# Moving the attention's loads to GpSimd's queue and its outputs to SyncE's, with an earlier copy and a later turn of the maxima

## The reference

```python
def reference(...):
    x = _layernorm(x + _L0_attn_ref(x, ...))      # sampled values, squeeze-excite gate, silu(out @ w_out)
    x = _layernorm(x + _L0_ffn_ref(x, ...))
    return x

def _L0_ffn_ref(x, ...):
    x = x + _msa(_layernorm(x, ln1_w, ln1_b), w_qkv, w_proj)
    x = x + _moe_mlp(_layernorm(x, ln2_w, ln2_b), gate_w, gate_b, w1, w2)
    return x

def _msa(x, w_qkv, w_proj):                       # 16 heads of 16 channels
    attn = softmax(q @ k.T / sqrt(16), axis=-1)
    return (attn @ v) @ w_proj
```

## Time and profile before

| | |
|---|---|
| median of three runs | 1563.61 us (1557.06 to 1567.67) |
| the profiled execution's own time | 1563.61 us |
| its span | 1561.0 us |
| granted PE clock, mean | 0.968 |
| busy share of the span: PE, DVE, ACT, POOL | 93%, 81%, 65%, 24% |
| attention block | 522 to 1189 us of the span |

### The profile page before, as it was taken

The page is one execution under the profiler, slowest core; times in us unless marked ns, Lnnn a source line. Parts: engine busy times, 40 slices in busy tenths (PEclk is TensorE's granted clock), DMA queues, the critical chain, the costliest instruction groups (busy, mean ns, idle before and its releaser), DMA issues. The chain is left out here.

```text
span 1561.0 us, 31581 instructions
## 1 busy us (share of the span) xinstructions
PE 1453.5 (93%) x11706; PEld 895.9 (57%) x11706; DVE 1264.0 (81%) x2433; ACT 1016.9 (65%) x1705; POOL 371.0 (24%) x633
## 2 busy tenths in 40 slices
PE   7688989998999999999999999999997769999997
PEld 7465656565655344444444444444444649999996
DVE  6889999964566799999999999999962867777773
ACT  3689999963433488888888888888885522222221
POOL 3011111103111012222222222222222732222222
PEclk9789999999999799999999999999998989999999
DMA  3300101014885544433444443443332775656561
GB/s 115 95 8 15 46 20 48 15 62 169 284 255 198 148 82 97 98 91 91 91 92 95 95 88 80 88 91 81 75 91 73 240 258 206 204 205 213 199 215 48
DMA packets 147303, 185.99 MB, mean 119 GB/s; under 512 B 68288, under 2 KB 99008, under 8 KB 147152
## 3 DMA queue, kind: packets, MB, share of 16 engines
q1 hardware_dynamic: 126896, 157.27, 35.8%
q0 software_dynamic: 19280, 26.46, 5.5%
q10 hardware_dynamic: 976, 0.24, 0.1%
HBM read 129.67 MB, written 54.21 MB: 118 GB/s over the span
## 5 line engine op out<-in xcount | busy, mean ns | idle before, releaser
L1684 ACT ACTIVATE at_p<-at_pst 128x512 f32<-128x512 f32 x1024 | 555.0, 597 | 101.8 <-PE at_pst L1732 82.5
L1696 DVE TENSOR_REDUCE at_mx<-at_pmx 128x2 f32<-128x1024 f32 x488 | 576.3, 1215 | 32.1 <-PE at_pmx L1723 29.6
L1748 PE MATMUL at_pacc<-at_p,at_v 128*32 128x256 f32 (+1 forms) x3840 | 324.1, 410 | 2.5 <-ACT at_p L1684 0.2
L1723 PE MATMUL at_pmx<-at_k,at_q 48*128 48x512 f32 x976 | 247.3, 503 | 2.8 <-PEq L1204 2.0
L1732 PE MATMUL at_pst<-at_q,at_k 50*128 50x512 f32 x1024 | 231.1, 409 | 5.1 <-ACT at_p L1684 5.0
L1723 PEld LDWEIGHTS at_pmx<-at_k,at_q 48*128 48x128 f32 x976 | 91.9, 185 | 213.8 <-issue 128.0
L878 PE MATMUL ws_pA<-ident,ws_A 128*128 128x128 f32 x1088 | 152.6, 288 | 23.9 <-ACT ws_A L660 21.6
L1732 PEld LDWEIGHTS at_pst<-at_q,at_k 50*128 50x128 f32 x1024 | 155.5, 188 | 30.4 <-ACT at_p L1684 24.2
L878 PEld LDWEIGHTS ws_pA<-ident,ws_A 128*128 128x128 f32 x1088 | 122.7, 146 | 84.1 <-ACT ws_A L660 37.7
L2251 DVE STREAM_TRANSPOSE ex_zr<-ex_row 32x64 f32<-32x64 f32 x608 | 143.2, 236 | 15.1 <-DMA ex_row<-scratch_routed 7.3
L1748 PEld LDWEIGHTS at_pacc<-at_p,at_v 128*32 128x32 f32 x3840 | 76.9, 108 | 131.4 <-ACT at_p L1684 83.9
(11 more groups left out here) (269 smaller groups left out, 1612.3 us busy)
## 6 DMA issues: line engine op xcount, KB each, us to landing
ex_w<-in_L_ffn_w SPq DMA_DIRECT2D x39, 1024.0 KB, 5.6
at_q<-scratch_qs SPq DMA_DIRECT2D x192, 64.0 KB, 3.1
at_k<-scratch_ks SPq DMA_DIRECT2D x192, 64.0 KB, 3.2
ex_row<-scratch_routed SPq DMA_DIRECT2D x39, 258.0 KB, 5.0
scratch_qs<-gp_split SPq DMA_DIRECT2D x16, 512.0 KB, 3.8
scratch_ks<-gp_split SPq DMA_DIRECT2D x16, 512.0 KB, 4.5
scratch_v<-gp_v SPq DMA_DIRECT2D x8, 1024.0 KB, 5.9
at_v<-scratch_v SPq DMA_DIRECT2D x32, 256.0 KB, 3.9
```

What stands on the lines that cost most here:

```text
L1684: a.activation(pt[:, n % BUFS, k % 2, :], pst[(w * 2 * STEPS + k) % BANKS][:], ACT.Exp).then_inc(exped, 1)
L1696: v.reduce_max(mx[w % 2][:].rearrange("p (h n) k -> p h n k", h=2)[:, :, j // 2, j % 2], pmx[n % SLOTS][:], AX.X).then_inc(taken, 1)
L1723: last = nc.tensor.matmul(pmx[n % SLOTS][:, h, :], att.rows(qst[u], h, ROWS)[:, nt * P:(nt + 1) * P], att.rows(kst[u], h, ROWS)[:, kh * HA ...
L1748: last = nc.tensor.matmul(out, vst[u][:, t, h, :], pt[:, n % BUFS - p + first:n % BUFS + 1, h, c * QUARTER:(c + 1) * QUARTER], start=(s == ...
```

## The change

It has these parts.

- The loads of q, k and v in `attention` move from SP's stream to POOL's. In `gate_and_project` the loads of units 0 and 1 stay on SP and count on semaphores of their own (`att.first`).
- `fold`, `spread` and `store` move from POOL's stream to SP's; `normalise` stays on POOL, behind the loads. SP's order in a unit is now `fold`, `load_w2` or `pad`, `spread`, `store_top`, `store`, all but `store_top` for the unit before. In the next block, `spread` and `store` of the last unit stand on SP ahead of the loads of chunks 2 and 3.
- `TURN` goes from 8 to 9, so `EARLY` from 16 to 14: at the end of `gate_and_project` there are 14 early maxima, spread 1, 1, 1, 1, 4, 4 over the six parts in place of 2, 2, 2, 2, 3, 3 (behind two ahead of them).
- `COPY` goes from 4 to 2.
- PE's wait for the rows of maxima stands ahead of the step's maxima matmuls.
- ACT's first exponential, SP's units and POOL's further loads wait until y0, v and the split q and k of all chunks are stored. The load of the Exp table at the end of `gate_and_project` moves behind the two copies of v.

The diff (only shifts of lines and repeated head lines are left out):

```diff
--- before.py
+++ after.py
@@ -1083,7 +1083,7 @@
     PIECES = 2 * BT
     MAXIMA = 2 * PIECES
     TOPS = 3
-    TURN = 8
+    TURN = 9
     Q = 32
     EARLY = 2 * (2 * BT - TURN)
     LOADS = 2 * 2 * len(STACK) * 16 + 16
@@ -1093,13 +1093,13 @@
 
         return a[h * self.BASE:h * self.BASE + n]
 
-    def load(self, eng, u, of_q, of_k):
+    def load(self, eng, u, of_q, of_k, loaded):
 
         for h in range(2):
             for n, (pq, pk) in enumerate(self.STACK):
                 at = slice(h * self.BASE + n * DK, h * self.BASE + (n + 1) * DK)
-                eng.dma_start(self.qst[u][at, :].bitcast(F32), of_q(pq, h)).then_inc(self.ld[u], 16)
-                eng.dma_start(self.kst[u][at, :].bitcast(F32), of_k(pk, h)).then_inc(self.ld[u], 16)
+                eng.dma_start(self.qst[u][at, :].bitcast(F32), of_q(pq, h)).then_inc(loaded, 16)
+                eng.dma_start(self.kst[u][at, :].bitcast(F32), of_k(pk, h)).then_inc(loaded, 16)
 
     def tops(self, dve, w):
 
@@ -1129,7 +1129,7 @@
     a.vst = [sb(f"at_v{i}", [P, BT, 2, 2 * DK]) for i in range(a.RING)]
     a.mx, a.top_ = [sb(f"at_mx{i}", [P, a.PIECES, 2]) for i in range(2)], sb("at_top", [P, a.PIECES])
     a.top2, a.turned = [sb(f"at_top2{i}", [P, a.Q], F32R) for i in range(2)], [sb(f"at_topT{i}", [P, a.Q]) for i in range(2)]
-    a.ld = [sem(f"at_load{i}") for i in range(a.RING)]
+    a.first, a.ld = [sem(f"at_first_load{i}") for i in range(2)], [sem(f"at_load{i}") for i in range(a.RING)]
     a.y0_out, a.v_out, a.split_out = sem("gp_y_out"), sem("gp_v_out"), [sem(f"gp_split_out{i}") for i in range(4)]
     a.one_rows, a.red, a.mxmm, a.topT, a.split = (sem("at_" + n) for n in ("ones", "reduced", "maxima", "topT", "top_split"))
     a.top_out, a.rows_in = sem("at_top_out"), sem("at_top_rows")
@@ -1233,9 +1233,9 @@
                 sp.wait_ge(att.one_rows, 2 * att.RING)
                 def part(d):
                     return lambda n, h: d[n, (2 * u + h) * DK:(2 * u + h + 1) * DK, 0:L]
-                att.load(sp, u, part(dr["qs"]), part(dr["ks"]))
+                att.load(sp, u, part(dr["qs"]), part(dr["ks"]), att.first[u])
                 sp.dma_start(att.vst[u][:].rearrange("p t h d -> p t (h d)"),
-                             dr["v"][0:L, u * (4 * DK):(u + 1) * (4 * DK)].rearrange("(t p) n -> p t n", p=P)).then_inc(att.ld[u], 16)
+                             dr["v"][0:L, u * (4 * DK):(u + 1) * (4 * DK)].rearrange("(t p) n -> p t n", p=P)).then_inc(att.first[u], 16)
 
             def chunk(i, prev):
                 if i + 1 < CHUNKS:
@@ -1323,9 +1323,9 @@
             ahead(a, chunk)
             for q in range(4):
                 top(CHUNKS - 1, q)
-            nc.scalar.activation(warm[:], hb2[:, 0:1], ACT.Exp)
             for q in range(4, 6):
                 values(CHUNKS - 1, q)
+            nc.scalar.activation(warm[:], hb2[:, 0:1], ACT.Exp)
 
         @block.vector
         def _(dve):
@@ -1401,9 +1401,8 @@
             peak(att.MAXIMA + 1)
             for q in range(4):
                 low(CHUNKS - 1, q)
-                peak(att.MAXIMA + 2 + 2 * q)
-                peak(att.MAXIMA + 3 + 2 * q)
-            for n in range(10, att.EARLY):
+                peak(att.MAXIMA + 2 + q)
+            for n in range(6, att.EARLY):
                 peak(att.MAXIMA + n)
 
         @block.gpsimd
@@ -1492,7 +1491,7 @@
                 w, m = n // att.MAXIMA, n % att.MAXIMA
                 nt, kh, h = m // 4, m // 2 % 2, m % 2
                 if m == 0:
-                    pe.wait_ge(att.ld[w], att.LOADS)
+                    pe.wait_ge(att.first[w], att.LOADS)
                 if w:
                     pe.wait_ge(silu3, CHUNKS)
                     if m >= 3:
@@ -1548,7 +1547,7 @@
             n = att.MAXIMA + 2
             for q in range(PARTS):
                 parts(CHUNKS - 1, q)
-                for _ in range(2 if q < 4 else 3):
+                for _ in range(1 if q < 4 else 4):
                     peak(n)
                     n += 1
 
@@ -1568,7 +1567,7 @@
     TOTAL = (UNITS - 1) * STEPS - EARLY
     BANKS, SLOTS, BUFS = 3, 2, 4
     LAG = 2
-    COPY = 4
+    COPY = 2
     INVERT = 6
 
     qst, kst, vst, mx = att.qst, att.kst, att.vst, att.mx
@@ -1595,18 +1594,6 @@
 
         @block.sync
         def _(sp):
-            def load(w):
-
-                b, pair, u = w // (H // 2), w % (H // 2), w % RING
-                if pair in (0, 2):
-                    for done in [att.v_out] + att.split_out:
-                        sp.wait_ge(done, 16 * (L // HALF) * (b + 1))
-                def part(d):
-                    return lambda n, h: d[n, (2 * pair + h) * DK:(2 * pair + h + 1) * DK, b * L:(b + 1) * L]
-                att.load(sp, u, part(dr["qs"]), part(dr["ks"]))
-                sp.dma_start(vst[u][:].rearrange("p t h d -> p t (h d)"),
-                             dr["v"][b * L:(b + 1) * L, pair * (4 * DK):(pair + 1) * (4 * DK)].rearrange("(t p) n -> p t n", p=P)).then_inc(ld[u], 16)
-
             def load_w2(w):
 
                 i, q, hc = w // RING, w % RING // 2, HID // P // 2
@@ -1625,26 +1612,29 @@
                 sp.dma_start(first.y0[:], dr["y0"][0:first.T * P, :].rearrange("(t p) c -> p t c", p=P)).then_inc(first.y0_in[0], 16)
 
             def unit(w):
-                if w and w + 3 < UNITS:
-                    sp.wait_ge(pv, w * STEPS)
-                    load(w + 3)
-                if w + 1 < UNITS:
-                    att.store_top(sp, w + 1)
+                if w:
+                    outputs.fold(sp, w - 1)
                 if w % 2:
                     load_w2(w)
                 elif 0 < w <= 2 * E:
                     pad(w // 2 - 1)
+                if w:
+                    outputs.spread(sp, w - 1)
+                if w + 1 < UNITS:
+                    att.store_top(sp, w + 1)
+                if w:
+                    outputs.store(sp, w - 1)
                 if w == UNITS - 2:
                     load_first()
 
-            load(2)
-            load(3)
             for dst, src in later:
                 sp.dma_start(dst, src).then_inc(later_in, 16)
-            sp.wait_ge(padded, 2)
+            for done in [att.y0_out, att.v_out] + att.split_out:
+                sp.wait_ge(done, 16 * CHUNKS)
+            sp.wait_ge(padded, 3)
             for w in range(UNITS):
                 unit(w)
-            sp.wait_ge(att.y0_out, 16 * CHUNKS)
+            outputs.fold(sp, UNITS - 1)
             sp.wait_ge(w_in, 16 * 2 * E)
             sp.wait_ge(pads_sent, 16 * E)
             sp.wait_ge(later_in, 16 * len(later))
@@ -1652,18 +1642,31 @@
         @block.gpsimd
         def _(pool):
             g = nc.gpsimd
+
+            def load(w):
+
+                b, pair, u = w // (H // 2), w % (H // 2), w % RING
+                def part(d):
+                    return lambda n, h: d[n, (2 * pair + h) * DK:(2 * pair + h + 1) * DK, b * L:(b + 1) * L]
+                att.load(g, u, part(dr["qs"]), part(dr["ks"]), ld[u])
+                g.dma_start(vst[u][:].rearrange("p t h d -> p t (h d)"),
+                             dr["v"][b * L:(b + 1) * L, pair * (4 * DK):(pair + 1) * (4 * DK)].rearrange("(t p) n -> p t n", p=P)).then_inc(ld[u], 16)
+
+            load(2)
+            load(3)
+            for done in [att.y0_out, att.v_out] + att.split_out:
+                pool.wait_ge(done, 16 * CHUNKS)
             g.memset(padrow[:], 0.0).then_inc(padded, 1)
             pool.wait_ge(padded, 1)
             g.iota(padrow[:, 2 * C:2 * C + 1].bitcast(I32), pattern=[[1, 1]], base=TOKENS, channel_multiplier=1,
                    allow_small_or_imprecise_dtypes=True).then_inc(padded, 1)
             g.memset(outputs.rd[:], 1.0).then_inc(padded, 1)
             pool.wait_ge(padded, 3)
-            for w in range(UNITS - 1):
-                outputs.fold(g, w)
-                outputs.spread(g, w)
-                outputs.normalise(g, w)
-                outputs.store(g, w)
-            outputs.fold(g, UNITS - 1)
+            for w in range(1, UNITS):
+                if w + 3 < UNITS:
+                    pool.wait_ge(pv, w * STEPS)
+                    load(w + 3)
+                outputs.normalise(g, w - 1)
 
         @block.scalar
         def _(a):
@@ -1674,7 +1677,8 @@
                     a.wait_ge(outputs.y_out[w % 2], w // 2 * outputs.MOVES)
                 a.copy(oe[w % 2][:], pacc[:]).then_inc(oed, 1)
 
-            a.wait_ge(att.y0_out, 16 * CHUNKS)
+            for done in [att.y0_out, att.v_out] + att.split_out:
+                a.wait_ge(done, 16 * CHUNKS)
             for w in range(UNITS):
                 for k in range(2 * STEPS):
                     n = w * STEPS + k // 2
@@ -1716,7 +1720,7 @@
             def maxima(w, j):
                 u, n, nt, kh = w % RING, nth(w, j), j // 2, j % 2
                 if j == 0:
-                    pe.wait_ge(ld[u], (w // RING + 1) * LOADS)
+                    pe.wait_ge(ld[u], ((w - 2) // RING + 1) * LOADS)
                 if n >= SLOTS:
```

(10 more changed lines are left out.)

## The result

The changed kernel takes 1577.91 us (median of 4, 1577.27 to 1599.09); the kernel before took 1560.34 on the same chip. The ratio is 1.0136, 95% interval 1.0088 to 1.0185: 1.4% slower, or some 21 us. The profiled execution took 1587.29 us (span 1585.4), the one of before 1563.61 (1561.0).

The account below looks back on a forecast made before the run. PE was taken to set the pace (busy 98.66 of 100 us in attention). From 1563.61 us, -6.9 + 0.6 + 1.0 + 0 + 1.8 + 0.8 + 0.3 = -2.4 gave 1561.2, range 1549 to 1580.

Parts of the forecast that it names:

- the third: Rows of maxima, attention units: TURN 9 puts tops 1.24 us later, a few late units, +1.0 us, bounds 0 and 15.5.
- rival A: Attention units: tops land only with the broadcast, rows 0.5 us late in each of 31 units, +15.5, 1575.7 us; chance 0.17.
- step 4: Attention units: loads of q, k and v on POOL cost nothing, bounds 0 and +1 us.
- The block's end: End of attention: last fold on SP lets PE start the next block sooner, -6.9 us, bounds 0 and -7.5.
- Rival C: End of attention: the gap is something every block change costs, so -6.9 goes, 1568.1 us; chance 0.08.
- The earlier copy: Boundary between units: COPY 2 costs +0.02 us per unit, +0.6 us over 31, bounds -7.4 to +7.8.
- Rival B: Boundary between units: the earlier copy is hidden, 31 x -0.24 = -7.4 us in place of +0.6, 1553.2 us; chance 0.09.
- The start: Start of attention: ACT's first exponential +2.3 us, PE's first values later, total +1.8 us, bounds 0 and +3.3.
- rival D: Start of attention: ten more steps at half clock, +9 us, 1570.2, or as much the other way; chance 0.06 over both.
- The tail: Last unit: load_first moves behind unit 29's stores and just fails to land in time, +0.8 us, bounds 0 and +2.
- The next block: After attention: chunk 2's load behind the spread's round trip, partly covered by PE's first projection, +0.3 us, bounds -2 and +2.

Follow-up runs that it names:

- e13: e11 with the spread (broadcast of the reciprocals) ahead of the tops on SP again; 1571.17 us, ratio 1.0088.
- e11: e8 with TURN 8, the order of the early maxima and the place of the Exp table load as before; 1555.87 us, ratio 0.9995.
- e7: The kernel before with the spread alone moved to SP, ahead of the tops; 1554.2 us, ratio 0.9979.
- e4: The kernel before with the last unit's fold alone on SP in place of POOL; 1547.16 us, ratio 0.9949.
- e14: e7 with TURN 9 and its order of the early maxima; 1560.47 us, ratio 1.001.
- e12: The kernel before with TURN 9 alone and the order of early maxima it needs; 1564.38 us, ratio 1.0052.
- e8: e1 with COPY 4, PROJECTED 8 and ACT waiting at the block's start for y0's stores alone; 1567.78 us, ratio 1.0065.
- e2: The changed kernel with TURN 8 and the early maxima as before; 1587.63 us, ratio 1.0186.
- e15: e11 with SP's load of chunk 2 ahead of the last spread in the next block; 1559.37 us, ratio 1.0027.
- e1: The changed kernel with the tops stored and loaded ahead of the spread on SP; 1569.16 us, ratio 1.0078.
- e6: e1 with PE's projection of the next block's first tiles at steps 8 to 14 of the last unit; 1568.16 us, ratio 1.0078.
- e9: e8 with the loads back on SP behind the fold, so POOL issues no DMA in the block; 1595.81 us, ratio 1.025.

## Why the prediction was wrong

I forecast 1561.2 and within 1% of the kernel before; it is 1577.9, 1.4% over it by the ratio. The step that failed is the third, the rows of maxima, taken at +1.0 us, "a few late units". Measured as e13 against e11, whose one difference is the order of broadcast and tops, it is +14.5. That is close to the 15.5 of its upper bound and of rival A, but only half by A's mechanism. A has each of 31 units 0.5 us late; in after 15 units take over 20.9 us, and behind two of the waits for the rows the clock falls, which I had counted only for the start; it makes two pairs of long units, 24.08 and 22.58, 23.30 and 27.35 us. That the total stands next to A's 1575.7 is luck, since A leaves all other steps as they are, and those missed as well.

The timetable was right in kind: tops, broadcast, row loads. It had two wrong entries. One is the tops' landing behind a broadcast, 4.56 us for 1.95, which I had put into rival A at 0.17 though both stood on one queue in the diff. Alone it costs nothing (e7). The other is how long the store of the reciprocals holds up the broadcast: 2.59 us in e7, 3.55 in after and 3.44 in e13. The two together pass the margin. In step 4 I had put the loads on POOL at "nothing", as `normalise` waits anyway; and that the weight piece now stands ahead of this store, in no step at all, though the change's list says it. The split in e13 puts 1.6 us on the units with a piece (4.07 for 2.44) and 0.4 on those without (3.02 for 2.63). The 0.4 may be the loads on POOL, where v's load of 256 KB goes out around the store, but fold and stores have moved to SP as well, and nothing separates them. The Trainium skill (DMA: Bandwidth & Descriptors, Queues, rings and completion order) says that a semaphore's increment lands only after the earlier writes of that DMA engine, across its queues; that fits the slower store, though no run here shows which transfer it waits for.

Point by point, the others:

1. The block's end: right in kind, -6.3 for -6.9, and -8.2 alone (e4). Its cover I had not seen: with 390 DMAs issued by POOL the next block opens no sooner than 9.89 us behind `normalise`. Whether that shows depends on how early `normalise` ends. With the broadcast ahead of the tops it ends 9.7 us ahead of the last copy in after and 8.3 in e13, whose last unit takes 20.6, and PE goes on 1.5 to 1.6 us behind the copy's end in both. With the tops first and a last unit of 20.6, in e11, it ends 3.5 us ahead, and the gap is 6.0 us again. So the cure of step 3 costs part of step 1. Rival C falls.
2. The earlier copy: +0.13 to 0.14 a unit, some 4 us in all, for +0.02 a unit. Inside the bounds of the step; both scores wait for ACT, and I had only the second. Rival B, the hidden copy, falls.
5. The start: ACT +2.5 for +2.3, `values` +2.3 for +1.8. The dear part was in kind rival D's: `TURN` 9 with its order of the early maxima costs 5 us (e14 against e7), 8 (e12) or, with the Exp table load moved too, 11 (e8 against e11). In e8 it is mostly the half clock in the first unit, 30.65 for 21.94 us; in e12 it mostly lies ahead of that unit. In ten profiles with the new order the first unit took 23.3 to 33.4 us nine times; with the old one and ACT's old wait 21.3 to 22.2 in five, 26.9 in the profile of before, which hid this cost when the two profiles are compared, and 29.5 in e2, which has the old order but ACT's new wait.
6. The tail: last unit 21.9 for 20.6 us, +1.3 for +0.8, but not for my reason. In after PE waits for no load there. It stands 0.77 us for ACT's exponential near the unit's start, where the kernels with `COPY` 4 show at most 0.3:

```profile
1196.21 0.99 PE L1736 MATMUL at_pst<-at_q,at_k 50*128 50x512 f32 x2 [0.77 <-ACT at_p L1688]
```

7. The next block: +4.1 (6.3 - 2.2) for +0.3. The projection of chunk 1 covers only part of the spread's round trip in SP's queue. Moving one load moves the wait to the next (e15), since the stores stand there too.

The measured parts, 14.5 for the rows, 5 to 11 for the start, 4 for the copy, 1.3 for the last unit, less 2.2 at the end, sum to some 23 to 29 us, against 21 by the ratio (17.6 by the two medians). They overlap: a unit that waits for the rows hides the copy, and the 14.5 already holds the gap of e11 that e13 hides. e1 and e13 bracket this; I have not separated it further. What stays open is the last unit of e1, 28.0 us, and of e6, 23.45. In e1 PE stood 2.12 us ahead of the first projection, and the clock was 0.66, 0.75 and 0.57 in three stretches of 5 us from 1170; in e6 it was 0.66 in one such stretch. How this divides between the late load and the earlier copy no run shows.

## What to carry to other kernels

Before a small DMA that somebody waits for is put behind a large one in the same queue, add the large one's landing to its time, and do the same for every store that triggers the large one; a margin that holds alone may fall to the second. List all that now stands ahead of such a store, also what the change seems only to pass by, as the weight piece here. Price a wait of a saturated TensorE not by its length alone but also by the clock it can cost: here four waits of ten were followed by 10 to 20 us at half clock. And a move that frees one engine's queue at a block's end is best made alone: the last fold on SP gave 8.2 us, and with all that was moved beside it the kernel is 17.6 us slower.

## What the hardware showed that I had not expected

- In after and e13 TensorE waited ten times for 1.1 to 1.6 us inside the attention block. Behind four of these waits (1.26, 1.44, 1.53 and 1.58 us) it ran at 1.2 GHz for 10 to 20 us though busy all the time; behind the other six (up to 1.49 us) it kept 2.4 GHz. At 1.2 GHz it was busy 5.00 of 5.00 us in three stretches of e13 and 10.00 of 10.00 in three of e8. The Trainium skill (TensorE: Matmul & The Clock Gate, Part 1) lets a busy array go back to full clock soon; these rows don't agree.
- GpSimd took 9.89 us from its last work to the next block in six kernels where it had issued 390 DMAs, 6.70 in before and e12 (218 DMAs), 4.49 in e7 and e14 (156), at most 3.23 in e9 (none). The last work was `normalise` in the six and in e9, an own DMA in the other four.
- A store of 16 KB took 1.95 us to its waiter alone, 4.6 us behind a broadcast of 256 KB in its own queue, and 2.1 to 2.4 with the broadcast in POOL's up to 0.3 us ahead; with it 1.3 us ahead there, once 3.87.
- A store of 8 KB (the reciprocals) took 2.44 us to its waiter in e7 and 4.07 in e13, where 512 KB of weights had gone out 4.9 us ahead in the same queue (medians of 14 units).
